# Macaron block on one core: both value halves of a unit behind the second score pair of the next

## The chip, the core and the metric

The kernel runs on one core of a Trainium2 chip. The metric is the device time of one execution in microseconds (us). The kernel before took 1315.32 us, the median of 3 runs between 1313.44 and 1316.38.

## What is computed

The reference is a macaron block over 4 batches of 1024 tokens with 128 features, all float32: half a mixture of experts, attention, half a mixture of experts again.

```python
x = x + 0.5 * _L0_ffn_ref(_layernorm(x), ...)      # 8 experts of 128 -> 512 -> 128, top 2
x = x + _L0_attn_ref(_layernorm(x), W_qkv, W_o)
x = x + 0.5 * _L0_ffn_ref(_layernorm(x), ...)

# attention: one projection serves as q, k and v; 16 heads of 8 features
qkv = (x @ W_qkv.T).reshape(b, n, H, DH).transpose(0, 2, 1, 3)
score = softmax(einsum('bhif,bhjf->bhij', qkv, qkv) / SQRT_D, axis=-1)
attn = einsum('bhij,bhjf->bihf', score, qkv)
out = attn.reshape(b, n, F) @ W_o.T
```

## The kernel before

Each of the five engines has its own program, written out by hand; semaphores tie them together. The change touches attention alone, and in it TensorE's program alone.

**Teams and units.** Four heads are a team; there are 4 teams in each of 4 batches, 16 in all. A team is worked in two halves of 512 queries, and a half in 8 units of 128 keys. A unit has four slots, one for each head; a slot is one score matrix of 128 keys by 512 queries. So a team is 64 slots (`TURN`), a half 32, and there are 1024 slots (`NSCORES`) and 256 units. TensorE issues slots in pairs: `tensor_scores` makes the two scores of a pair at once, in the upper and lower 64 rows of the array (L2245, L2249). A unit therefore has a first pair (slots 0 and 1 of it) and a second pair (slots 2 and 3).

**Row maxima.** For a softmax without overflow the maximum of each query's row is needed before its scores are made. `tensor_row_max` makes scores in the other orientation, 128 queries by 512 keys for two heads at once, in two banks (L2228, L2229), and VectorE reduces them (L1959, one instruction over both banks; L1964, one for each bank, where the two aren't neighbours). There are 512 such maxima of two banks; 26 are made ahead of the first score, and then one stands behind each score pair until they are used up. The last 26 pairs of slots have none: this is called the tail of attention here.

**Exponentials and values.** ScalarE turns each score bank into probabilities in `probs`, which holds 8 slots, two units (L1445). `tensor_values(n, part)` multiplies the probabilities of unit n with the values of its four heads, for half of the queries at a time (`part` 0 and 1): for each part 4 matmuls side by side in the columns of the array, each written as 2 instructions, so 8 matmuls of L2267 for a part. They add into one bank, `value_bank`, over the 8 units of a half; after a half ScalarE copies it out (L1460).

**The ring of banks.** Seven of the eight banks of PSUM are handed out in turn by `Ring` (`att_bank`): in program order each score takes one, each maximum two, and each chore that needs a bank one. The writer of a bank waits until the one that held it seven banks earlier is emptied (`empty_before`): by ScalarE (`by_act`) for a score or a chore, by VectorE (`reduced`) for a maximum. The order in which banks are handed out is scores, maxima, chores for each pair of slots; the values don't appear in it.

**Chores.** Side work is planned by slot (`chores[slot]`) and is issued by every engine behind the pair with that slot: "place" (the maxima of a half are transposed by TensorE, L2284, and written where the scores take them in), "finish" (the copied value bank, transposed by TensorE, L2290, copied by ScalarE, L1465, and divided by the sums on VectorE, L1987 and L1989), "rows" (L2296, L2303: transposes and the output projection of a batch's half), "prepare" (the next batch's normalisation and projection) and "route" (the routing of the second mixture of experts). With the slots counted from the start of a half, place stands behind slot 15 of a half, the bank's copy behind slot 3, the finish transposes behind slot 6, rows behind slots 14 and 16.

**What orders the values.** In the loop of `tensor_attention` part 0 of unit n - 1 stands behind the first pair of unit n and part 1 behind its second pair, ahead of the chores. Part 0 waits until the last exponential of its unit is made, and at the first unit of a half until the bank of the half before is copied out; part 1 raises `valued`. ScalarE's first exponential of a unit waits on `valued` for the unit two before. Behind the loop the last unit's two parts follow each other.

Of the kernel before, what the change touches and what calls it, by code (L numbers as in the profile page):

```python
# [90 lines left out]
def build_macaron(nc, x, w_qkv, w_o, ln_g, ln_b, router_w, eg, eb, w1, b1, w2, b2, wo, bo, out):  # L91
# [81 lines left out]
    UNIT = TEAM  # L173
# [6 lines left out]
    with stack:  # L180
# [360 lines left out]
        def when_emptied(name):  # L541
            return banks_of(name).emptied(name)
# [37 lines left out]
        def max_units(slot):  # L580
            return range(max_upto[slot - 1] if slot else MAX_FIRST, max_upto[slot])
# [25 lines left out]
        for n in range(1, PLACINGS):  # L607
            slot = next(s for s in range(NSCORES) if max_upto[s] >= min((n + 1) * HALF_UNITS + 2, MAX_UNITS))
# [1433 lines left out]
        def tensor_program():  # L2042
            for what, which, step, part in first_routing():
                if what == "route":
                    tensor_route(which, step, part)
                elif what == "fold":
                    tensor_fold(which)
            tensor_experts(0)
            tensor_attention()
            tensor_experts(1)  # L2050
# [144 lines left out]
        def tensor_attention():  # L2195
            TE.wait_ge(weighed, BLOCKS)
            TE.wait_ge(combined, HC * BLOCKS)
            TE.wait_ge(turn_copied, BLOCKS)
            for n in range(MAX_FIRST):
                tensor_row_max(n)  # L2200
                if n == HALF_UNITS + 1:
                    for chore in first_chores:
                        tensor_chore(*chore)
            for slot in range(0, NSCORES, 2):
                tensor_scores(slot)
                for n in max_units(slot + 1):
                    tensor_row_max(n)
                if slot >= UNIT:
                    tensor_values(slot // UNIT - 1, slot % UNIT // 2)
                for chore in chores[slot] + chores[slot + 1]:  # L2210
                    tensor_chore(*chore)
            for part in range(2):
                tensor_values(NSCORES // UNIT - 1, part)

        def tensor_row_max(n):
            i, g, p, t, keys = max_of(n)
            s = i % OPERANDS
            if n == i * 2 * HALF_UNITS:
                if i < OPERANDS:
                    TE.wait_ge(max_rows_set, i + 1)  # L2220
                TE.wait_ge(lefts_in[s], lefts_before(i))
                TE.wait_ge(rights_in[s], rights_before(i))
            for emptied in att_bank.empty_before(("max", n)):
                TE.wait_ge(*emptied)
            low, high = max_banks(n)
            q = slice((g * HT + t) * P, (g * HT + t + 1) * P)
            k = slice(keys * HALF, (keys + 1) * HALF)
            TE.matmul(bank[low], left[s][PRODUCTS[0], p, q], right[s][PRODUCTS[0], p, k], start=True, stop=True)  # L2228
            TE.matmul(bank[high], left[s][PRODUCTS[1], p, q], right[s][PRODUCTS[1], p, k],  # L2229
                      start=True, stop=True).then_inc(maxed, 1)  # L2230

        def tensor_scores(slot):

            i, at = divmod(slot, TURN)
            u, j = divmod(at, UNIT)
            half, kt = divmod(u, BT)
            s, p = i % OPERANDS, j // 2
            if kt == 0 and j == 0:
                TE.wait_ge(max_in[s], 16 * 2 * (placed_before(2 * i + half) + 1))
            low, high = ring_bank(("score", slot)), ring_bank(("score", slot + 1))  # L2240
            k = slice(kt * P, (kt + 1) * P)
            q = slice(half * HALF, (half + 1) * HALF)
            for emptied in att_bank.empty_before(("score", slot)):
                TE.wait_ge(*emptied)
            TE.matmul(low, left[s][WITH_MAX[0], p, k], right[s][WITH_MAX[0], p, q],  # L2245
                      start=True, stop=True).then_inc(att_bank.filled, 1)
            for emptied in att_bank.empty_before(("score", slot + 1)):
                TE.wait_ge(*emptied)
            TE.matmul(high, left[s][WITH_MAX[1], p, k], right[s][WITH_MAX[1], p, q],  # L2249
                      start=True, stop=True).then_inc(att_bank.filled, 1)  # L2250

        def tensor_values(n, part):

            i, u = divmod(n, UNITS)
            half, kt = divmod(u, BT)
            b, team = divmod(i, TEAMS)
            if part == 0:
                TE.wait_ge(*when_emptied(("prepare", b, 15)))
                if kt == 0:
                    if 2 * i + half:  # L2260
                        TE.wait_ge(value_copied, 2 * i + half)
                    else:
                        TE.wait_ge(value_bank_blanked, 1)
                TE.wait_ge(*att_bank.emptied(("score", UNIT * (n + 1) - 1)))
            q = slice(part * HALF // 2, (part + 1) * HALF // 2)
            for j, head in enumerate(HEAD_OF):
                last = TE.matmul(value_bank[head * VS:head * VS + VW, q], values[:, b % 2, kt, team * TEAM + head, :],  # L2267
                                 probs[:, (UNIT * n + j) % PROBS, q],
                                 start=(kt == 0 and part == 0), stop=(kt == BT - 1 and part == 1))
            if part == 1:  # L2270
                last.then_inc(valued, 1)
# [99 lines left out]
```

## Time and profile before

| | |
|---|---|
| median of 3 runs | 1315.32 us |
| the profiled execution's own time | 1316.4 us |
| its span in the profile | 1314.7 us |
| mean granted TensorE clock | 0.975 |
| TensorE busy (matmuls) | 1157.7 us, 88% |
| VectorE busy | 1135.0 us, 86% |
| ScalarE busy | 889.2 us, 68% |
| GpSimd busy | 470.5 us, 36% |

The profile is of one execution. PE is TensorE, PEld its weight loads, DVE VectorE, ACT ScalarE, POOL GpSimd. In the timeline a row is one or several like instructions in a row: start, how long they last together, engine, line, what is written and read, their count, and in square brackets how long the engine was idle before them and who ended that. Instructions of one engine overlap in part: the next of a kind starts before the last has ended, so that the distance of two starts, and not the length of one, is the beat. A granted clock of 1.00 is 2.4 GHz, 0.50 is 1.2 GHz. The first mixture of experts takes the span up to some 340 us, attention runs to 1070 us, the second mixture follows.

### The profile page before, as it was taken

The page shows a single profiled execution, that of the slowest core. Times are in us where ns is not written, and L with a number is a line of the kernel's source. Part 1 is how long each engine was busy: PE and PEld are TensorE (multiplying, and loading weights), DVE is VectorE, ACT ScalarE, POOL GpSimd, SP SyncE. Part 2 cuts the span into 40 slices and gives each one's busy share as a digit, 9 for nine tenths or more (in the row PEclk, how much of TensorE's full clock was granted, in tenths as well). Part 3 has the DMA queues.
Part 4 walks back from the last instruction along what each step waited for, and adds up shares of the span by engine and source line. Part 5 has one row for each costly group of instructions (what it writes and reads, how often), then busy time and mean ns, then how long its engine had stood idle before and what let it go on. Part 6 is the DMA issues. An engine that isn't in the chain of part 4 may idle for free.

```text
span 1314.7 us, 27184 instructions
## 1 busy us (share of the span) xinstructions
PE 1157.7 (88%) x9031; PEld 635.2 (48%) x9031; DVE 1135.0 (86%) x2367; ACT 889.2 (68%) x1879; POOL 470.5 (36%) x515
## 2 busy tenths in 40 slices
PE   3847999888599999999999999999998889999993
PEld 2746888777123333333323233233322258778882
DVE  7877888887899999989998999999999468988885
ACT  1224555555178999898888888888887965555651
POOL 3873547343113001314225313333333117643222
PEclk9999999999589999999999999999999999999997
DMA  8125565554010200002001000001000403554653
GB/s 275 52 70 184 204 208 188 218 214 130 28 34 19 66 15 6 18 20 64 2 28 37 12 28 18 18 27 27 18 5 22 176 33 120 207 195 178 255 201 138
DMA packets 58616, 123.54 MB, mean 94 GB/s; under 512 B 12352, under 2 KB 33826, under 8 KB 58448
## 3 DMA queue, kind: packets, MB, share of 16 engines
q1 hardware_dynamic: 49488, 103.83, 23.0%
q0 software_dynamic: 8704, 16.93, 4.1%
q8 instruction: 75, 1.23, 0.4%
q10 hardware_dynamic: 288, 1.05, 0.2%
q14 instruction: 61, 0.50, 0.1%
HBM read 36.66 MB, written 23.88 MB: 46 GB/s over the span
## 4 chain that ended last, share of the span: by engine, by line
PE 51%; DVE 29%; POOL 6%; issue 5%; ACT 4%; DMA 4%; SPq 1%; DVEq 0%; POOLq 0%; ACTq 0%
DVE att_neg_part L1959 15%; PE psum L2267 12%; PE psum L2181 7%; PE psum L2245 7%; PE psum L2169 7%; PE psum L2171 6%; PE psum L2228 4%; POOL rows_dram L1252 4%; DVE att_neg_part L1964 3%; DMA ffn_block_rows<-rows_dram 2%; DVE stats L1593 2%; DVE ffn_x2c L1900 2%; ACT att_probs L1445 1%; DVE ffn_hidden L1911 1%; PE psum L2121 1%
## 5 line engine op out<-in xcount | busy, mean ns | idle before, releaser
L1445 ACT ACTIVATE att_probs<-psum 128x512 f32<-128x512 f32 x1024 | 555.4, 599 | 59.3 <-PE psum L2249 30.8
L1959 DVE TENSOR_REDUCE att_neg_part<-psum 128x2 f32<-128x1024 f32 x443 | 520.2, 1217 | 32.2 <-PE psum L2229 30.4
L2267 PE MATMUL psum<-att_probs,att_values 128*16 128x256 f32 x4096 | 322.4, 387 | 12.4 <-ACT att_o_t L1460 7.7
L1413 ACT ACTIVATE ffn_silu<-ffn_x2c,ffn_rec 128x256 f32<-128x256 f32 (+1 forms) x320 | 154.7, 487 | 169.3 <-DVE ffn_x2c L1900 168.1
L1268 POOL DMA_INDIRECT y_dram<-ffn_y,ffn_block_rows x144 | 142.4, 989 | 234.5 <-ACT ffn_y L1431 206.3
L2249 PE MATMUL psum<-att_right,att_left 64*128 64x512 f16 x512 | 199.7, 390 | 18.8 <-DVE att_neg_part L1959 13.2
L2228 PE MATMUL psum<-att_right,att_left 62*128 62x512 f16 x512 | 199.3, 390 | 16.3 <-DVE att_neg_part L1959 11.7
L2245 PE MATMUL psum<-att_right,att_left 64*128 64x512 f16 x512 | 199.6, 390 | 8.1 <-DVE att_neg_part L1959 6.7
L2229 PE MATMUL psum<-att_right,att_left 62*128 62x512 f16 x512 | 200.9, 393 | 0.0
L1900 DVE TENSOR_SCALAR ffn_x2c<-psum,ffn_rec 128x256 f32<-128x256 f32 (+1 forms) x320 | 162.6, 512 | 35.9 <-PE psum L2171 31.8
L2169 PE MATMUL psum<-ffn_block_t,ffn_rec 128*128 128x256 f32 (+1 forms) x640 | 178.6, 361 | 1.2 <-ACT ffn_block_t L1364 1.2
L2171 PE MATMUL psum<-ffn_block_t,ffn_rec 128*128 128x256 f32 (+1 forms) x640 | 177.6, 359 | 0.0
L1252 POOL DMA_INDIRECT rows_dram<-rows,place_i x128 | 127.1, 993 | 131.5 <-PE psum L2249 62.6
L2267 PEld LDWEIGHTS psum<-att_probs,att_values 128*16 128x16 f32 x4096 | 69.2, 94 | 191.1 <-issue 132.1
L1911 DVE SCALAR_TENSOR_TENSOR ffn_hidden<-psum,ffn_rec,ffn_silu 128x256 f32<-128x256 f32 (+1 forms) x320 | 144.0, 450 | 18.9 <-ACT ffn_silu L1413 16.8
L2181 PE MATMUL psum<-ffn_hidden,ffn_rec 128*128 128x256 f32 (+1 forms) x640 | 141.3, 364 | 11.5 <-DVE ffn_hidden L1919 11.4
L2245 PEld LDWEIGHTS psum<-att_right,att_left 64*128 64x128 f16 x512 | 47.3, 92 | 203.9 <-ACT att_probs L1445 128.6
L2181 PEld LDWEIGHTS psum<-ffn_hidden,ffn_rec 128*128 128x128 f32 x640 | 111.5, 191 | 31.8 <-DVE ffn_hidden L1919 19.1
L2171 PEld LDWEIGHTS psum<-ffn_block_t,ffn_rec 128*128 128x128 f32 x640 | 117.2, 191 | 13.5
L2169 PEld LDWEIGHTS psum<-ffn_block_t,ffn_rec 128*128 128x128 f32 x640 | 111.5, 192 | 12.1 <-ACT ffn_block_t L1364 1.8
L1172 POOL TENSOR_TENSOR att_max_parts<-att_max_rest,att_max_parts 16x128 f16<-16x128 f32 x32 | 13.4, 420 | 286.4 <-ACT att_max_parts L1514 286.4
L1964 DVE TENSOR_REDUCE att_neg_part<-psum 128x1 f32<-128x512 f32 x138 | 88.2, 680 | 4.8 <-PE psum L2229 4.3
(236 smaller groups left out, 1171.6 us busy)
## 6 DMA issues: line engine op xcount, KB each, us to landing
ffn_rec<-record SPq DMA_DIRECT2D x80, 776.5 KB, 3.8
ffn_block_rows<-rows_dram SPq DMA_DIRECT2D x64, 130.0 KB, 3.1
record<-in_L_ffn_W SPq DMA_DIRECT2D x16, 256.0 KB, 6.5
att_left<-q_parts_dram SPq DMA_DIRECT2D x64, 64.0 KB, 2.2
y_dram<-ffn_y,ffn_block_rows POOLq DMA_INDIRECT x144
x_sb<-in_L_attn_x SPq DMA_DIRECT2D x4, 512.0 KB, 7.1
record<-in_L_ffn_Wo SPq DMA_DIRECT2D x8, 256.0 KB, 7.0
rows_dram<-rows,place_i POOLq DMA_INDIRECT x128, 2.4
```

The source lines that it names most:

```text
L1252: G.indirect_dma_start(rows_dram[k_ffn][:, :], bass.IndirectOffsetOnAxis(ap=r.place_i[:, k, t:t + 1], axis=0), r.rows[:, t, k, :], None).t ...
L1445: S.activation(probs[:, slot % PROBS, :], ring_bank(("score", slot))[:, :], ACT.Exp, scale=unlift).then_inc(att_bank.by_act, 1)
L1900: V.tensor_scalar(mix[k].x2c[:, n % 2, few], chunk_bank[n % 4][:, few], mix[k].rec[:, s, CLIP_LO + c:CLIP_LO + c + 1], mix[k].rec[:, s, CL ...
L1959: last = V.tensor_reduce(out=neg_part[:, h % 2, keys, p::PAIR, t], in_=psum[:, low:high + 1, :], axis=AX.X, op=ALU.max, negate=True)
L2169: TE.matmul(both[:, few], mix[k].rec[:, s, W2 + c * P:W2 + (c + 1) * P], mix[k].block_t[:, m % 2, few], start=True, stop=True)
L2171: TE.matmul(both[:, w1_few], mix[k].rec[:, s, W1 + c * P:W1 + (c + 1) * P], mix[k].block_t[:, m % 2, few], start=True, stop=True).then_inc ...
L2181: last = TE.matmul(y_bank[n % 2][:, few], mix[k].rec[:, s, WO + c * F:WO + (c + 1) * F], mix[k].hidden[:, n % 2, c, few], start=(c == 0), ...
L2228: TE.matmul(bank[low], left[s][PRODUCTS[0], p, q], right[s][PRODUCTS[0], p, k], start=True, stop=True)
L2229: TE.matmul(bank[high], left[s][PRODUCTS[1], p, q], right[s][PRODUCTS[1], p, k], start=True, stop=True).then_inc(maxed, 1)
L2245: TE.matmul(low, left[s][WITH_MAX[0], p, k], right[s][WITH_MAX[0], p, q], start=True, stop=True).then_inc(att_bank.filled, 1)
L2249: TE.matmul(high, left[s][WITH_MAX[1], p, k], right[s][WITH_MAX[1], p, q], start=True, stop=True).then_inc(att_bank.filled, 1)
L2267: last = TE.matmul(value_bank[head * VS:head * VS + VW, q], values[:, b % 2, kt, team * TEAM + head, :], probs[:, (UNIT * n + j) % PROBS, ...
```

## The change

Both parts of the value products of a unit are issued behind the second pair of the next unit, in one run, where part 0 stood behind the first pair and part 1 behind the second. The order of the ring of banks, the chores and the other engines' programs stay as they are.

```diff
                 tensor_scores(slot)
                 for n in max_units(slot + 1):
                     tensor_row_max(n)
-                if slot >= UNIT:
-                    tensor_values(slot // UNIT - 1, slot % UNIT // 2)
+                if slot >= UNIT and slot % UNIT == UNIT - 2:
+                    for part in range(2):
+                        tensor_values(slot // UNIT - 1, part)
                 for chore in chores[slot] + chores[slot + 1]:
                     tensor_chore(*chore)
```

## Rows read from the trace of the kernel before

**Rows 1.** The page's first part: busy us, share of span, instructions.

```profile
PE 1157.7 (88%) x9031; PEld 635.2 (48%) x9031; DVE 1135.0 (86%) x2367; ACT 889.2 (68%) x1879; POOL 470.5 (36%) x515
```

**Rows 2.** Busy us by stretch: PE, PEld, DVE, ACT, POOL, granted clock, DMA share, GB/s.

```profile
340.00:364.00 24.00, 12.87 (x44) 2.75 (x42) 23.86 (x26) 1.71 (x3) 0.42 (x1) 0.50 0.16 45
364.00:1033.00 669.00, 630.82 (x6178) 204.60 (x6177) 628.63 (x904) 582.69 (x1137) 189.45 (x201) 0.99 0.09 24
```

**Rows 3.** Groups by line, 364 to 1033 us: busy us, mean ns | idle before.

```profile
L1959 DVE TENSOR_REDUCE att_neg_part<-psum 128x2 f32<-128x1024 f32 x424 | 498.2, 1217 | 30.0 <-PE psum L2229 28.2
...
L2228 PE MATMUL psum<-att_right,att_left 62*128 62x512 f16 x486 | 184.3, 379 | 3.5 <-DVE att_neg_part L1959 2.6 <-DVE att_neg_part L1964 0.5
L1964 DVE TENSOR_REDUCE att_neg_part<-psum 128x1 f32<-128x512 f32 x130 | 83.2, 681 | 4.8 <-PE psum L2229 4.3
```

**Rows 4.** Timeline of TensorE in a steady stretch.

```profile
442.20 0.39 PE L2245 MATMUL psum<-att_right,att_left 64*128 64x512 f16 x1
...
442.42 0.38 PE L2228 MATMUL psum<-att_right,att_left 62*128 62x512 f16 x1
...
443.29 0.39 PE L2245 MATMUL psum<-att_right,att_left 64*128 64x512 f16 x1
```

**Rows 5.** Timeline of VectorE, two stretches of attention.

```profile
475.50 1.23 DVE L1959 TENSOR_REDUCE att_neg_part<-psum 128x2 f32<-128x1024 f32 x1 [0.41 <-PE psum L2229]
...
477.13 1.22 DVE L1959 TENSOR_REDUCE att_neg_part<-psum 128x2 f32<-128x1024 f32 x1
...
478.47 1.22 DVE L1959 TENSOR_REDUCE att_neg_part<-psum 128x2 f32<-128x1024 f32 x1
...
486.53 6.87 DVE L1959 TENSOR_REDUCE att_neg_part<-psum 128x2 f32<-128x1024 f32 x6
...
545.13 0.48 DVE L1593 BATCH_NORM_STATS2 stats<-x_sb 128x6 f32<-128x128 f32 x2
...
545.92 2.36 DVE L1959 TENSOR_REDUCE att_neg_part<-psum 128x2 f32<-128x1024 f32 x2
```

**Rows 6.** Timeline around the place transpose L2284 at 420.44 us.

```profile
419.94 1.09 ACT L1445 ACTIVATE att_probs<-psum 128x512 f32<-128x512 f32 x2
...
420.65 0.39 PE L2245 MATMUL psum<-att_right,att_left 64*128 64x512 f16 x1
...
421.17 0.37 PE L2228 MATMUL psum<-att_right,att_left 62*128 62x512 f16 x1
...
421.22 1.05 ACT L1445 ACTIVATE att_probs<-psum 128x512 f32<-128x512 f32 x2
421.50 0.62 PE L2267 MATMUL psum<-att_probs,att_values 128*16 128x256 f32 x8
421.60 2.36 DVE L1959 TENSOR_REDUCE att_neg_part<-psum 128x2 f32<-128x1024 f32 x2 [0.38 <-PE psum L2229]
...
422.06 0.39 PE L2249 MATMUL psum<-att_right,att_left 64*128 64x512 f16 x1
...
422.48 0.60 ACT L1445 ACTIVATE att_probs<-psum 128x512 f32<-128x512 f32 x1 [0.21 <-PE psum L2249]
```

**Rows 7.** Timeline at the finish transposes and at the output projection.

```profile
454.77 0.65 PE L2290 MATMUL psum<-identity,att_o_t 128*128 128x128 f32 x4
...
455.36 0.39 PE L2245 MATMUL psum<-att_right,att_left 64*128 64x512 f16 x1
...
455.95 1.09 ACT L1445 ACTIVATE att_probs<-psum 128x512 f32<-128x512 f32 x2
...
698.76 1.16 PE L2303 MATMUL psum<-wo_t,att_xh_t 128*128 128x128 f32 x8
```

**Rows 8.** Timeline of TensorE at the end of attention.

```profile
1068.84 1.06 PE L2267 MATMUL psum<-att_probs,att_values 128*16 128x256 f32 x16 [0.28 <-ACT att_probs L1445]
1069.83 0.44 PE L2121 MATMUL psum<-identity,ffn_block_rows 128*128 128x128 f32 x2
```

**Rows 9.** Timeline of TensorE in the tail, two units.

```profile
1037.87 0.62 PE L2267 MATMUL psum<-att_probs,att_values 128*16 128x256 f32 x8 [0.39 <-ACT att_probs L1445]
...
1040.08 0.62 PE L2267 MATMUL psum<-att_probs,att_values 128*16 128x256 f32 x8 [0.39 <-ACT att_probs L1445]
```

## What the change was predicted to do

> **What bounds the kernel now.** I read the page's totals first, then the table by stretches, the groups by line inside attention, and last the timeline of a few microseconds at a time. VectorE is busy 86% of the span and TensorE 88% [rows 1], so neither average settles it. The change touches only attention. There the scores run from 364 to 1033 us, 669 us, and a tail without row maxima follows to 1070 us. In the 669 us VectorE is busy for 628.6, TensorE for 630.8 and ScalarE for 582.7 [rows 2]. Of VectorE's idle time 34.8 us lie before its row maxima, 32.5 of them ended by a TensorE matmul [rows 3].
>
> A steady stretch shows the beat [rows 4]. Scores at 442.20, maxima 0.22 us later, the next scores at 443.29: 1.10 us for a pair of slots. The value half stands between: 0.32 us from the maxima to it, 0.56 from it to the scores (421.17, 421.50, 422.06) [rows 6]. VectorE takes six maxima in 6.87 us; with 1.22 for the last that is 1.13 each [rows 5]. So a unit (two pairs) is 2.26 us of VectorE, 2.2 us of TensorE. VectorE is the bound, TensorE is 0.05 us behind it, and whenever TensorE has side work (transposes of a finished half, say) VectorE stands for 0.4 us and more [rows 5, 6]. ScalarE has room: a queued exponential follows the last in about 0.5 us (two in 1.09, where one lasts 0.60) [rows 6].
>
> **Part by part: the switches that go.** The same value matmuls run before and after; nothing is added, no DMA moves, and the queues of SyncE and GpSimd are untouched. Only where TensorE issues the first value half differs. The price of one run of both halves stands in the trace once, at the very end, where the last unit's halves already follow each other: 16 matmuls start at 1068.84 and the next kind starts at 1069.83, 0.99 us, against 0.56 for 8 [rows 8, 6]. So the second half costs 0.43. A value run also costs 0.10 in front: maxima to values take 0.32, scores to maxima 0.22, for the same 512 columns [rows 6, 4]. A unit thus falls from 2.20 to 0.22 + 0.22 + 0.22 + 0.32 + 0.99 = 1.97 us of TensorE, 0.23 less.
>
> The Trainium skill has a rule that explains that gap (TensorE: Matmul & The Clock Gate, Part 3, what overlaps): a weight load runs beside matmuls in flight only where its row group differs. By that rule alone one run per unit is a gain; it is the first rival below.
>
> **The wait that comes.** The seven banks are handed out in one order: score, score, maximum (two banks), and so on. Counting seven banks back, the maximum pair of pair p takes the banks of the second maximum bank of pair p-2 and of the first score of pair p-1. So the maxima of a unit's second pair may not start before the exponential of its first pair's first score has ended. Today nobody notices: pairs are 1.1 us apart, maxima 0.22 later, 1.32 in all. The release is worth: scores to exponential 0.42 (422.06 to 422.48), exponential 0.60, its end to the waiting matmul 0.14, together 1.16 us. The 0.14 is from a place where such a wait shows now, behind the small transpose L2284, which also takes a bank: exponentials at 419.94 and about 0.49 later, the second over at 421.03, L2228 at 421.17 [rows 6]. That matmul waited 0.52 us behind its scores instead of 0.22, so the counting of banks holds.
>
> After the change the value halves stand behind the second pair. Its maxima wait to 1.16 us after the first pair's scores, then come 0.32 to the values (421.17 to 421.50 [rows 6]) and 0.99 for the run, and only then the next unit's scores. Nothing in this loop overlaps: 1.16 + 0.32 + 0.99 = 2.47 us a unit. TensorE's own 1.97 are not the bound, nor VectorE's 2.26, the loop is, 0.21 us slower than VectorE. Two other waits are met. The first exponential of a unit needs the value products of two units before: a run of 16 ends 0.07 us after the next scores may start (1.06 against 0.99 [rows 8]), the exponential starts 0.42 after them. And the values need the last exponential of the unit before, which ends about when the new unit's scores start, 1.4 us earlier.
>
> A second rule of the skill agrees (Perfetto Trace Analysis, identifying the most-contended engine): the same gap repeated on the engine that should be full can mean too few PSUM buffers. No row here shows such a gap on VectorE yet.
>
> **The sum for the 669 us.**
> First, 243 units (486 maxima [rows 3]) at 2.47: 600 us.
>
> Second, side work behind a second pair lies in the loop in full. By their slots the place transposes and the finish transposes all do, 30 of each in the stretch (one for each 16 maxima). Place: 0.21 on TensorE and 0.15 by which ScalarE is late for the next exponential (421.22 for 421.07) [rows 6]; 0.36 x 30 = 11. Finish: 454.77 to 455.36 is 0.59, ScalarE late by 0.17 (455.95 for 455.78) [rows 7]; 0.76 x 30 = 23. The copy of the value bank on ScalarE, which now waits for a run that ends later, I estimate at the same 0.17: 5. Sum 39.
>
> Third, the other side work (rows, prepare and route chores). Behind a second pair it costs its length and 0.17, behind a first only what goes over 1.16 - 0.75 = 0.41 us (TensorE would be back at 0.22 + 0.22 + 0.10 + 0.22, about 0.75). L2303 (some 1.1 us [rows 7], six times by its slots, all behind a first pair) costs 0.7 each, 4. L2296, transposes like those of the finish and six times behind a second pair, costs 5. The rest, some twenty, stands by its slots half and half; at 0.76 behind a second pair, little behind a first, and more for the 16 router matmuls, about 17. Sum 26, between 12 and 32.
>
> Fourth, VectorE's own other work. 424 maxima at 1.13 and 65 split ones, two halves of 0.68 that overlap, at an estimated 1.20 [rows 3, 5] are 557 us; 628.6 - 557 = 72. Of it the finish steps (475.50 to 477.13 is 1.63, 0.50 over a maximum) and neg_max (477.13 to 478.47, 0.21 over) are 21, inside units that the second point already stretches. The other 51 come in packets of 0.79 (545.13 to 545.92) [rows 5], so some 64 units are 3.05 us of VectorE, above the loop by 0.58 each: 37.
>
> Off that go units that have both of the last two, about 4, and VectorE's lag of up to 0.35 us, which after a packet carries one or two light units, about 6. The first two units, at the low clock, add about 1.
>
> 600 + 39 + 26 + 37 - 10 + 1 = 693, against 669: 24 slower. **The tail** has no maxima. Its unit is 2.21 us (1037.87 to 1040.08) because the values behind a first pair wait 0.39 for an exponential [rows 9]; that wait goes, and ScalarE could do a unit in about 2.0. But much of the tail is the chain of the last routing's side work, which crosses all engines, so I take 1 us of gain.
>
> The profiled execution took 1316.4 us, 1.7 over its span and 1.1 over the median of 1315.3. 1316.4 + 24 - 1 = 1339.
>
> **Rivals.**
> - The switches decide (faster). The ring's wait doesn't bind, TensorE saves 0.23 x 243 = 56 us, and VectorE can give back at most its 34.8 idle. Half of that, since side work behind the values now comes 0.43 later: about 1300. For it: every VectorE gap follows TensorE work [rows 3]. Against it: it needs the loop under 2.26, that is 0.21 out of five measured terms. Chance 0.08.
> - VectorE's backlog covers. Split maxima, packets and lag fill more of the units than I counted, or the loop is 2.37 and not 2.47: 24 us less for the units, 6 more for the packets, 1321, and 1314 to 1325 around it. For it: half of the units carry something besides two plain maxima. Chance 0.12.
> - All side work is exposed and nothing comes back: 600 + 39 + 32 + 37 + 1 = 709, 40 slower, and no gain in the tail: 1356. Chance 0.18. In it lies the low clock too. TensorE would idle 0.5 us of a light unit (2.47 - 1.97), where it hardly idles now. The granted clock was 0.50 from 340 to 364 us with TensorE busy for 12.9 of 24, 0.99 behind it with 630.8 of 669 [rows 2]; a fifth of idle time lies nearer to the second, but isn't excluded.
> - The same matmuls run, so the change does nothing: possible only where VectorE covers; it is inside the second rival.
>
> **The numbers.** Forecast 0.62, at 1339, between 1328 and 1350. The range leaves out the faster rival, the low end of the second and the half of the third that lies above 1356: 1316 to 1356. A measurement here can tell about 0.2% (2.6 us) from no change. Faster 0.09, within 0.2% 0.05, slower 0.86.
>
> **What would show it.** Right: L2228 of every second pair idles before it for an exponential, some 0.3 to 0.7 us; 16 value matmuls in one row, 0.99 to the next scores; VectorE idle about 0.2 us before the maxima of a first pair; light units of 2.47 us where six maxima in a row take 6.87 us now [rows 5]. Wrong: a light unit at 2.26 us, or L2228 starting 0.22 behind its scores in both pairs, or a run of 16 well off 0.99.

## The result, and the profile after

The changed kernel took 1342.94 us (median of 4 runs, 1341.72 to 1347.59), the kernel before beside it 1314.8: 1.0222 of it, 95% interval 1.0201 to 1.0244. The profiled execution is the slowest of the four, 1347.6 us with a span of 1345.9.

The stretches say where the time came in. The table by stretches of the changed kernel (columns as in [rows 2]) has the scores with maxima up to 1061 us:

```profile
364.00:1060.00 696.00, 618.27 (x6162) 227.44 (x6162) 638.09 (x901) 563.93 (x1136) 189.19 (x201) 0.99 0.08 24
...
1096.00:1345.90 249.90, 218.80 (x1137) 186.72 (x1134) 200.18 (x509) 124.99 (x319) 101.47 (x100) 0.94 0.48 173
```

| from the trace, us | before | after |
|---|---|---|
| first score pair | 363.5 | 364.4 |
| first score pair without a maximum | 1032.9 | 1061.1 |
| stretch with maxima (243 units) | 669.4 | 696.6 |
| last values to the second mixture | 1069.8 | 1096.0 |
| tail of attention | 36.9 | 34.9 |
| second mixture of experts | 244.8 | 249.9 |

27.2 us came in the stretch, 2.0 went in the tail. The 5 us of the second mixture are hardly the change's: nothing in it differs, and in the experiments below it is 244.7 to 254.8 us without relation to attention's order (244.8 in the ring of six banks, which has the changed order). They are as much as the profiled execution lies above its median (4.7 us); the other three executions have no trace to compare.

TensorE is less busy in the stretch than before (618 of 696 us against 631 of 669 in [rows 2]), as it should be with half the switches, and yet slower. The groups by line, 364 to 1060 us, show what it does instead (busy, mean ns | idle before, releaser), to be read against [rows 3]; the change shifted the lines by one:

```profile
L1959 DVE TENSOR_REDUCE att_neg_part<-psum 128x2 f32<-128x1024 f32 x423 | 503.3, 1221 | 45.4 <-PE psum L2230 37.4
...
L2229 PE MATMUL psum<-att_right,att_left 62*128 62x512 f16 x487 | 184.2, 378 | 42.1 <-ACT att_probs L1445 36.6 <-DVE att_neg_part L1959 1.1
...
L1964 DVE TENSOR_REDUCE att_neg_part<-psum 128x1 f32<-128x512 f32 x130 | 83.4, 683 | 7.1 <-PE psum L2230 5.8
```

TensorE idled for 3.5 us in all before its first maximum matmul (L2228); now, at L2229, it idles for 42.1, and 36.6 of them end with ScalarE's exponential. VectorE stands for 52.5 us before its maxima (45.4 + 7.1), not 34.8. One light unit of the timeline has the whole loop, TensorE and ScalarE:

```profile
490.09 0.39 PE L2246 MATMUL psum<-att_right,att_left 64*128 64x512 f16 x1
490.10 0.39 PE L2250 MATMUL psum<-att_right,att_left 64*128 64x512 f16 x1
490.32 0.38 PE L2229 MATMUL psum<-att_right,att_left 62*128 62x512 f16 x1
490.32 0.38 PE L2230 MATMUL psum<-att_right,att_left 62*128 62x512 f16 x1
490.52 2.06 ACT L1445 ACTIVATE att_probs<-psum 128x512 f32<-128x512 f32 x4 [0.41 <-PE psum L2250]
490.54 0.38 PE L2246 MATMUL psum<-att_right,att_left 64*128 64x512 f16 x1
490.68 0.39 PE L2250 MATMUL psum<-att_right,att_left 64*128 64x512 f16 x1
491.26 0.37 PE L2229 MATMUL psum<-att_right,att_left 62*128 62x512 f16 x1 [0.19 <-ACT att_probs L1445]
491.27 0.39 PE L2230 MATMUL psum<-att_right,att_left 62*128 62x512 f16 x1
491.58 1.06 PE L2268 MATMUL psum<-att_probs,att_values 128*16 128x256 f32 x16
492.57 0.39 PE L2246 MATMUL psum<-att_right,att_left 64*128 64x512 f16 x1
```

First pair's scores at 490.09, its maxima at 490.32, second pair's scores already at 490.54. Its maxima come only at 491.26, 1.17 us after the first pair's scores. Then 0.32 to the values, 0.99 for the run of 16, next unit at 492.57: 2.48 us. 99 of the 243 units take just that, to 0.01 us; most of the others carry side work or VectorE's other work.

### The profile page after: what moved, and what is told of

It is laid out like the page before. It is cut to its first block, busy times and chain, and to the rows that moved or that the text cites. A ratio compares the mean times of both kernels' runs of the same rounds, so it can differ in the third digit from the quotient of the medians.

```text
span 1345.9 us, 27184 instructions
## 1 busy us (share of the span) xinstructions
PE 1147.0 (85%) x9031; PEld 662.5 (49%) x9031; DVE 1144.9 (85%) x2367; ACT 870.1 (65%) x1879; POOL 469.7 (35%) x515
## 4 chain that ended last, share of the span: by engine, by line
PE 46%; DVE 32%; ACT 7%; issue 6%; POOL 5%; DMA 3%; SPq 1%; DVEq 0%; POOLq 0%; ACTq 0%
DVE att_neg_part L1959 17%; PE psum L2268 11%; PE psum L2181 7%; PE psum L2169 6%; PE psum L2171 6%; ACT att_probs L1445 5%; PE psum L2229 5%; PE psum L2246 4%; POOL rows_dram L1252 4%; DVE att_neg_part L1964 3%; DMA ffn_block_rows<-rows_dram 2%; DVE ffn_x2c L1900 2%; DVE stats L1593 2%; DVE ffn_hidden L1911 1%; PE psum L2291 1%
## 5 line engine op out<-in xcount | busy, mean ns | idle before, releaser
L1445 ACT ACTIVATE att_probs<-psum 128x512 f32<-128x512 f32 x1024 | 534.5, 605 | 79.6 <-PE psum L2250 56.5
L1959 DVE TENSOR_REDUCE att_neg_part<-psum 128x2 f32<-128x1024 f32 x443 | 526.4, 1221 | 47.1 <-PE psum L2230 39.1
L2268 PE MATMUL psum<-att_probs,att_values 128*16 128x256 f32 x4096 | 273.0, 384 | 3.3 <-ACT att_probs L1445 3.3
L2229 PE MATMUL psum<-att_right,att_left 62*128 62x512 f16 x512 | 197.8, 387 | 54.9 <-ACT att_probs L1445 36.6
L2250 PE MATMUL psum<-att_right,att_left 64*128 64x512 f16 x512 | 197.3, 389 | 23.9 <-DVE att_neg_part L1959 18.2
L2246 PE MATMUL psum<-att_right,att_left 64*128 64x512 f16 x512 | 195.9, 386 | 12.1 <-DVE att_neg_part L1959 8.6
L2268 PEld LDWEIGHTS psum<-att_probs,att_values 128*16 128x16 f32 x4096 | 94.5, 96 | 121.1 <-issue 49.9
L2246 PEld LDWEIGHTS psum<-att_right,att_left 64*128 64x128 f16 x512 | 47.3, 94 | 138.5 <-ACT att_probs L1445 55.7
L2229 PEld LDWEIGHTS psum<-att_right,att_left 62*128 62x128 f16 x512 | 48.2, 94 | 122.6 <-issue 52.3
```

The lines of the kernel that those rows point to most:

```text
L1445: S.activation(probs[:, slot % PROBS, :], ring_bank(("score", slot))[:, :], ACT.Exp, scale=unlift).then_inc(att_bank.by_act, 1)
L1959: last = V.tensor_reduce(out=neg_part[:, h % 2, keys, p::PAIR, t], in_=psum[:, low:high + 1, :], axis=AX.X, op=ALU.max, negate=True)
```

## The experiments

Two theories were set against each other. One: the unit is set by a loop, scores, exponential of slot 0, release of its bank, second maxima, value run, next scores. Two: the long value run itself starves VectorE, or an engine is short of throughput. A light unit is one with nothing on any engine beside its four slots and two maxima; its length, as the distance of two value runs or of two units' first scores, tells them apart better than the whole time does. The two kernels themselves were compared at 1314.8 us for the kernel before. Of the experiments, the first four in the table ran on a chip on which the kernel before took 1326.41 us, the last three on one where it took 1315.16; so ratios and stretches are compared, not times. Each stretch is from one profiled execution. An expectation given as a whole time was made for a chip at 1315.

| kernel | median, us | ratio to before (95%) | stretch, us | light unit, us: expected, measured |
|---|---|---|---|---|
| before | 1314.8 | 1 | 669.4 | 2.21 to 2.26 |
| changed | 1342.94 | 1.022 (1.020 to 1.024) | 696.6 | 2.47, 2.48 |
| both parts behind the first pair | 1385.71 | 1.045 (1.041 to 1.049) | 724.2 | 2.64, 2.64 |
| exponential of slot 0 halved | 1331.48 | 1.003 (1.001 to 1.006) | 677.2 | 2.26 to 2.30, 2.26 to 2.39 |
| exponential of slot 1 halved | 1352.01 | 1.020 (1.017 to 1.024) | 697.4 | 2.47, 2.48 |
| changed, maxima halved | 1313.17 | 0.991 (0.987 to 0.995) | 669.4 | 2.47, 2.48 |
| before, maxima halved | 1248.27 | 0.949 (0.946 to 0.951) | 612.4 | 2.20 to 2.21, 2.21 |
| ring of six banks | 1431.38 | 1.088 (1.085 to 1.091) | 785.7 | 2.97, 2.96 |
| run only beside side work | 1313.42 | 0.9982 (0.9969 to 0.9995) | 665.1 | as before, 2.21 to 2.26 |

**The run at another place.**

```diff
-                if slot >= UNIT and slot % UNIT == UNIT - 2:
+                if slot >= UNIT and slot % UNIT == 0:
```

> Both value parts of a unit stand in one run behind the FIRST score pair of the next unit instead of the second; nothing else differs from the changed kernel. Same run of 16, same number of switches on TensorE, another wait in the loop. Theory (a loop through ScalarE sets the unit): behind the first pair the values themselves wait for the last exponential of the unit before: 0.42 + 0.49 + 0.60 + 0.14 = 1.65 us after the second pair's scores, then 0.99 for the run, and only then the next second pair: 2.64 us a light unit against 2.48 in the changed kernel. Side work behind a second pair is now nearly hidden, so the whole comes out near the changed kernel: about 1346 us, 1335 to 1360; the mark is the light unit. Rival (the long run itself, wherever it stands, is what starves VectorE): light units of 2.48 as in the changed kernel, and the whole within 5 us of 1343.

Timeline of TensorE and ScalarE, one light unit and the start of the next:

```profile
649.61 0.39 PE L2246 MATMUL psum<-att_right,att_left 64*128 64x512 f16 x1
...
650.03 2.07 ACT L1445 ACTIVATE att_probs<-psum 128x512 f32<-128x512 f32 x4 [0.58 <-PE psum L2250]
...
651.26 1.06 PE L2268 MATMUL psum<-att_probs,att_values 128*16 128x256 f32 x16
652.25 0.39 PE L2246 MATMUL psum<-att_right,att_left 64*128 64x512 f16 x1
```

The second pair's scores stand at 649.61, the values 1.65 us later, the next second pair's scores 0.99 after that: 2.64 us, the expected loop to the hundredth, with the same run of 16. So the run alone doesn't set the unit; the wait in series with it does. The whole missed its range: 724.2 us in the stretch, where the expectation's 1346 stands for about 700, and 1.045 is 1374 on a chip at 1315, not 1335 to 1360. The units round the finish transposes show one cause. The same kernel's timeline there:

```profile
656.98 1.06 PE L2268 MATMUL psum<-att_probs,att_values 128*16 128x256 f32 x16 [0.53 <-ACT att_o_t L1460]
...
658.51 0.66 PE L2291 MATMUL psum<-identity,att_o_t 128*128 128x128 f32 x4
659.10 0.39 PE L2246 MATMUL psum<-att_right,att_left 64*128 64x512 f16 x1
...
659.63 0.37 PE L2229 MATMUL psum<-att_right,att_left 62*128 62x512 f16 x1
...
659.95 1.06 PE L2268 MATMUL psum<-att_probs,att_values 128*16 128x256 f32 x16
```

The side work behind the second pair was held to be nearly hidden. It isn't: it takes a bank of the ring, so the next maxima wait (659.63, 0.53 behind their scores instead of 0.22), and the values before it wait 0.53 for the copied value bank. From one second pair's scores to the next, the unit with that wait takes 3.08 us, the one with the finish transposes 2.97, and one with a place transpose alone 2.97. Over 2.64 that is 0.44 + 0.33 + 0.33 = 1.10 us a half, 33 us in 30 halves, about as much as in the changed kernel (1.16 a half, below). How much of the missing 24 us this is can't be said, because the expectation named no number for side work. The rest I haven't taken apart.

**The exponential that is waited for, and the one that isn't.** Half of the probabilities of one slot in four are not computed.

```diff
-                    S.activation(probs[:, slot % PROBS, :], ring_bank(("score", slot))[:, :], ACT.Exp,
+                    few = slice(0, HALF // 2 if slot >= PROBS and slot % UNIT == 0 else HALF)
+                    S.activation(probs[:, slot % PROBS, few], ring_bank(("score", slot))[:, few], ACT.Exp,
```

> The changed kernel, but ScalarE's exponential of slot 0 of each unit (the one that the maxima of the second pair wait for) works on 256 of its 512 queries, from the third unit on; half of those probabilities are not computed. Theory (ring wait on that exponential): it falls from 0.60 to about 0.33 us, the loop from 2.47 to 2.20, under VectorE's 2.26; light units go back to 2.26 to 2.30 us, TensorE's idle time before the second pair's maxima nearly goes. 0.2 us in some 175 units is 35 us: about 1308, 1298 to 1320. Rival 1 (run or switches starve VectorE): no change, 1343. Rival 2 (ScalarE is short of throughput): faster, but e3 by as much.

The other kernel has `slot % UNIT == 1` in the first added line.

> The changed kernel, but the exponential of slot 1 of each unit is halved instead of slot 0's: the same work is taken off ScalarE, at a place where no maxima wait for it. Theory (only the first slot's exponential is in the loop): light units stay at 2.47, the whole at 1343, at most 4 us less. Rival (ScalarE's throughput): as much faster as with slot 0's halved, some 35 us.

Same work taken off ScalarE, another slot. Slot 0: from 1.022 to 1.003 of the kernel before, and the intervals are far apart. Slot 1: 1.020, the changed kernel's own ratio. That rules out ScalarE's throughput and leaves the release of slot 0's bank. Timeline of TensorE with slot 0 halved, two value runs, and between them the scores of both pairs and the second maxima:

```profile
533.28 1.06 PE L2269 MATMUL psum<-att_probs,att_values 128*16 128x256 f32 x16
534.27 0.39 PE L2247 MATMUL psum<-att_right,att_left 64*128 64x512 f16 x1
...
534.71 0.38 PE L2247 MATMUL psum<-att_right,att_left 64*128 64x512 f16 x1
535.22 0.37 PE L2230 MATMUL psum<-att_right,att_left 62*128 62x512 f16 x1
535.54 1.06 PE L2269 MATMUL psum<-att_probs,att_values 128*16 128x256 f32 x16
```

The second maxima now stand 0.95 us behind the first pair's scores (1.17 above), and the unit shown is 2.26, which is VectorE's two maxima as well. Not every light unit gets there: 2.26 is the most frequent length, and most of the rest take 2.32 to 2.39. The gain was put too high: 35 us were expected, and 19.4 came in the stretch (696.6 to 677.2); 1.003 is 1319 on a chip at 1315, where 1308 was expected. 0.003 over the kernel before stay, 7.8 us in the stretch. Light units account for some 3 of them (68 units at 2.31 on average, 2.27 in the kernel before). The rest isn't taken apart; no run shows the side work behind the long run by itself.

**VectorE taken out of the way.** Each maximum is taken over half of its keys; the matmuls are whole.

```diff
-                last = V.tensor_reduce(out=neg_part[:, h % 2, keys, p::PAIR, t], in_=psum[:, low:high + 1, :],
+                last = V.tensor_reduce(out=neg_part[:, h % 2, keys, p::PAIR, t], in_=psum[:, low:high + 1, 0:HALF // 2],
...
-                    last = V.tensor_reduce(out=neg_part[:, h % 2, keys, PAIR * k + p, t:t + 1], in_=bank[where],
+                    last = V.tensor_reduce(out=neg_part[:, h % 2, keys, PAIR * k + p, t:t + 1], in_=bank[where][:, 0:HALF // 2],
```

> The changed kernel, with every row maximum taken over 256 of the 512 keys of each bank (half of the reduction is left out; the matmuls run whole). VectorE's beat falls from 1.13 to about 0.65 us. Theory (the loop TensorE - ScalarE - TensorE doesn't contain VectorE): light units stay at 2.47, packets of VectorE work fall under the loop, so 243 x 2.47 + 39 + 26 = 665 in the stretch, 31 less than now: about 1312, 1300 to 1320. Rival (VectorE sets the pace in the changed kernel too): light units fall to TensorE's own 1.97, 1220 or less.

> The kernel before, with every row maximum taken over 256 of the 512 keys of each bank, as in the run on the changed kernel. Theory: with VectorE out of the way the kernel before runs at TensorE's beat, 2.20 to 2.21 us a unit, and side work on TensorE adds some 44: 243 x 2.2 + 44 = 580 in the stretch against 669, so about 1227, 1215 to 1245. Together with the same cut in the changed kernel: the difference between the two orders grows from 28 to some 85 us, because VectorE covered most of the loop. Rival (the one run saves switches and is limited by VectorE alone): the changed order is the faster of the two once VectorE is light.

With the changed order light units stay at 2.48 although VectorE now stands idle for a good part of each (two value runs of the timeline):

```profile
605.76 1.06 PE L2268 MATMUL psum<-att_probs,att_values 128*16 128x256 f32 x16
608.24 1.06 PE L2268 MATMUL psum<-att_probs,att_values 128*16 128x256 f32 x16
```

So VectorE isn't in the loop. The stretch is 669.4 us where 665 were expected. The ratio of 0.991 comes from ahead of it: 26 maxima are made before the first score, and with them halved it starts at 358.3 us, against 369.8 to 373.2 in the other three experiments of that chip (351.5 against 364.2 and 367.3 for the old order). The expectations left out these 12 to 16 us. With the old order the beat is TensorE's 1.10 to 1.11 us a pair. The stretch is 612.4, not 580, and the whole, 1248.27, lies just outside 1215 to 1245 in spite of the earlier start. 243 light units are 537 us, so 75 are left for side work where the expectation had 44. The timeline of that kernel shows one thing that it left out:

```profile
594.10 0.59 ACT L1460 COPY att_o_t<-psum 128x512 f32<-128x512 f32 x1
...
594.79 0.63 PE L2267 MATMUL psum<-att_probs,att_values 128*16 128x256 f32 x8 [0.38 <-ACT att_o_t L1460]
...
596.44 0.66 PE L2290 MATMUL psum<-identity,att_o_t 128*128 128x128 f32 x4
```

In the old order the first values of a half wait for the copy of the bank before, 0.38 us here, in the unit that also has the finish transposes, so it takes 3.23 us (26 times), 1.02 over a light one. The difference of the two orders is 57 us in the stretch without VectorE's cover and 27 with it: VectorE hid half of the loss. I had expected 85 against 28. The order with one run isn't faster even with a light VectorE (669.4 against 612.4), which ends the rival of the saved switches.

**One bank less.**

```diff
-        att_bank = Ring(7, semaphore("bank_full"), semaphore("bank_emptied"), maxed, reduced)
+        att_bank = Ring(6, semaphore("bank_full"), semaphore("bank_emptied"), maxed, reduced)
```

> The changed kernel with a ring of six banks instead of seven. Theory: counting six banks back, the maxima of the second pair wait for the exponential of slot 1 instead of slot 0, one beat of ScalarE (0.49) later: the light unit goes from 2.48 to 2.97 us, and 0.49 in the units that VectorE doesn't cover makes 90 us: about 1433, 1405 to 1460. Rival (the maxima of the second pair don't hang on the ring but on TensorE's queue): a smaller loss, of the maxima waiting for VectorE, and no step of 0.49 in the light unit.

```profile
560.64 0.37 PE L2229 MATMUL psum<-att_right,att_left 62*128 62x512 f16 x1 [0.83 <-ACT att_probs L1445]
...
563.60 0.37 PE L2229 MATMUL psum<-att_right,att_left 62*128 62x512 f16 x1 [0.83 <-ACT att_probs L1445]
```

2.96 us from one second maximum to the next, and the idle time before it is 0.83. With seven banks it was 0.34 in the kernel with halved maxima, where nothing but the exponential holds TensorE up there, and 0.19 in the changed kernel, where the scores before it had waited too. 0.83 - 0.34 = 0.49 is one beat of ScalarE more, which is what counting back six banks instead of seven says. The stretch grew by 89 us, where 90 were expected. A ring of eight wasn't tried: the eighth bank holds the values.

**A mix of both orders.** In a unit with TensorE side work behind its first pair and none behind its second, both parts stand behind the second; everywhere else one behind each.

```diff
-                if slot >= UNIT:
-                    tensor_values(slot // UNIT - 1, slot % UNIT // 2)
+                if slot >= UNIT:
+                    for part in parts_behind(slot):
+                        tensor_values(slot // UNIT - 1, part)
...
+        def parts_behind(slot):
+            first = slot - slot % UNIT
+            if side_work(first) and not side_work(first + 2):
+                behind_second = (0, 1)
+            else:
+                behind_second = (1,)
+            return behind_second if slot % UNIT else [part for part in range(2) if part not in behind_second]
```

> The kernel before, but in those units in which TensorE has side work behind the first pair and none behind the second (output projection, one part of prepare and route), both value parts stand behind the second pair; all other units keep one part behind each. In such a unit VectorE now stands 0.96 us behind the side work; with the values moved away the maxima come 0.55 us earlier, and the next ones some 0.4 later. Theory: 0.1 to 0.3 us gained in each of some 15 units, 1312 to 1315, not to be told from the kernel before (1315). Rival (one run per unit saves its 0.23 and more wherever the loop is covered): 4 us or more faster.

1313.42 us and 0.9982 of the kernel before (0.9969 to 0.9995, 12 executions against 17): 4 us shorter in the stretch of the one trace, 1.7 in the median, at the edge of what can be told. The rival's 4 us and more are not in the median. It is the only order here that isn't slower than the kernel before.

## Why the prediction was right, point by point

- **The wait that comes.** Forecast a loop of 1.16 + 0.32 + 0.99 = 2.47 us; measured 1.17 + 0.32 + 0.99 = 2.48, and two loops that the experiments built from the same parts came out as worked out ahead (2.64, and 2.96 for 2.97). With the shorter exponential the loop was put at 2.20 and is 0.95 + 0.32 + 0.99 = 2.26. The step that carried it was counting the banks of the ring back in program order and then asking how far apart writer and releaser would stand in the new order, not how long they had waited in the old one: before, all waits at that matmul together took 3.5 us [rows 3].
- **The switches that go.** The run of 16 takes 0.99, as in its one instance [rows 8]. TensorE is 12.5 us less busy over the stretch. Worth nothing in time.
- **Side work behind the second pair** (39 us forecast). In the kernel with halved maxima, where VectorE hides nothing, the units of a quiet half are 2.48, with 3.26 at the finish transposes, 2.65 behind them and 2.69 at the place transpose: 0.78 + 0.17 + 0.21 = 1.16 a half, 35 us in 30. Forecast were 1.29; ScalarE's lateness behind the place transpose (0.15) didn't count. The 0.17 for the copy of the value bank was a guess by likeness, and no run shows that share alone.
- **Other side work** (26, between 12 and 32). 669.4 - 243 x 2.48 - 35 = 32: the upper end. This is what the other terms leave over and not a measurement of that work, and the low clock's 1 us is in it.
- **VectorE's packets** (37, less 10). 696.6 - 669.4 = 27, what VectorE adds to the loop: the total is just that. Its making isn't as drawn: of 33 units in which VectorE alone has other work, 12 still take 2.48, and the 33 take 2.80 on average, not 3.05.
- **The tail** (1 us gained): 2.0. A unit falls from 2.21 to 1.91 us, as from one values run of this timeline to the next. The values' wait for an exponential, which the forecast let go, is still there: 0.31 us, not 0.39. The tail's end is the routing chain, with a wait of 2.15 us in it:

```profile
1067.78 1.06 PE L2268 MATMUL psum<-att_probs,att_values 128*16 128x256 f32 x16 [0.31 <-ACT att_probs L1445]
...
1069.69 1.06 PE L2268 MATMUL psum<-att_probs,att_values 128*16 128x256 f32 x16 [0.31 <-ACT att_probs L1445]
...
1091.28 0.18 PE L2111 MATMUL psum<-chosen,before 128*128 128x32 bf16 x1 [2.15 <-DVE ratio L1671]
```

- **The sum.** 24 slower in the stretch was forecast, 27.2 measured; 1339 in all against 1342.94. That it came so near is in part luck: the units came out 3 us over the forecast, the side work behind the second pair 4 under and the other side work 6 over. And the 1339 started from the profiled execution of the kernel before, 1.1 us over its median. Of the change itself, 23 us were forecast and 28.1 measured between the medians.
- **Where it was off.** The marks: idle time before the second maxima was to be 0.3 to 0.7 us and is 0.19, because the second pair's second score matmul (L2250) itself waits for VectorE's release (490.68, 0.14 behind L2246 at 490.54) and fills part of it. In the kernel with halved maxima that wait is gone, and the idle time before the second maxima is 0.34. And VectorE's 0.2 us before a first pair's maxima show only as 0.12: the reduction starts 1.34 us behind the one before, not 1.13, but a reduction that doesn't follow at once no longer overlaps with the one before, and the lost 0.08 of overlap count as busy time. The maxima's busy time rose by 5.3 us for the same work [rows 3], of the 9.5 by which VectorE's rose (628.6 to 638.1). Both are the size of a mark, not of a term.
- **The low clock** of the third rival didn't come: 0.99 in the stretch, as before.
- **The two rules of the Trainium skill.** One says that a weight load runs beside matmuls in flight only with another row group (TensorE: Matmul & The Clock Gate, Part 3). The prediction took it to explain the 0.10 us that a value run costs in front. The changed kernel's timeline bears the 0.10 but not the rule as it stands:

```profile
490.09 0.39 PE L2246 MATMUL psum<-att_right,att_left 64*128 64x512 f16 x1
...
490.11 0.10 PEld L2229 LDWEIGHTS psum<-att_right,att_left 62*128 62x128 f16 x1
...
491.58 0.56 PEld L2268 LDWEIGHTS psum<-att_probs,att_values 128*16 128x16 f32 x16 [0.23 <-issue]
```

  The values' weights are loaded only when their run starts. But the weights of L2229 are loaded while L2246 runs in the same upper rows. What makes the 0.10 stays open. Saving it moved nothing, because TensorE wasn't what the unit waited for. The other rule takes a gap that repeats on the engine that should be full as a possible sign of too few PSUM buffers (Perfetto Trace Analysis; it stands there under Optimization Strategy, not where the prediction put it). The trace agrees: VectorE's gap of 0.12 repeats in each light unit, and a bank less made the unit 0.48 us longer.

## What to carry to other kernels

Where engines pass buffers round a ring, moving work within one engine's program moves it against every release: count the ring back from each instruction in the new order and add up the longest cycle of waits and work. Here it was 2.48 us against the 2.26 of the busiest engine, and that difference in the uncovered units, with the side work that lay in the cycle, made most of the loss. Batching the value products saved time on TensorE alone; in this kernel it paid nothing in the stretch with maxima, because the others didn't wait for TensorE's work but for a release.

## What the runs showed of the hardware

- A queued exponential of 128x512 lasts 0.60 us and the next starts 0.49 behind it; for another engine that waits on it the 0.60 count and 0.14 more until its matmul starts. 0.74 is half as much again as 0.49, and it is the longer one that stands in a loop. Halving its 512 columns took it from 0.61 to 0.39 us and brought the second maxima 0.22 us nearer, not the 0.27 that had been expected.
- The value products of both halves in one run took 0.99 us where two runs take 1.12, and 0.10 us of switch in front came once instead of twice.
- The second mixture of experts, in which no kernel here differs, took 244.7 to 254.8 us from one profiled execution to another: 10 us that a comparison of whole profiled times would charge to attention.
